# Tree-path attention with a chosen linear layer, four sequences on one core: halves in the first chain, early loads, and denominators summed ahead on VectorE

## The reference, cut to what matters

```python
# 1 conditioned bottleneck, 64 wide, one weight set per sequence
w_down = down_project * (cond @ down_gamma) + cond @ down_beta
h = relu(x @ w_down) @ (up_project * (cond @ up_gamma) + cond @ up_beta) + x
# 2 attention: 8 heads, similarity = shared prefix of 5 soft decisions
paths = sigmoid(h @ Wp + bp)                       # [.., 8 heads, 5]
agree = pq * pk + (1 - pq) * (1 - pk)
sim = cumprod(agree, -1).sum(-1) / 5               # causal mask
x = x + softmax(sim) @ (h @ Wv) @ Wo
# 3 hypernetwork layer, weight of rank 30 per sequence
U = (cond @ W_dec + b_dec).reshape(257, 30)
z = x @ (U @ V)[:-1] + (U @ V)[-1]
# 4 add one of 8 expert products, chosen per token
x = x + z + (z @ expert_w[argmax(z @ gate_w.T)].T)
```

## Time and profile before

| | us |
|---|---|
| median of 3 runs | 155.72 (155.0 to 155.99) |
| the profiled execution | 155.55 |
| its span | 153.4 |
| TensorE busy | 141.2 (92%) |
| VectorE busy | 83.7 (55%) |
| ScalarE busy | 58.8 (38%) |
| GpSimd busy | 31.2 (20%) |

### The profile page before, as it was taken

How to read it: one execution, slowest core, us unless ns; L and a number is a source line. 1 busy time by engine, 2 the same in 40 slices (tenths; PEclk the granted TensorE clock), 3 DMA queues, 4 the chain that set the end, 5 groups by cost and what they waited for, 6 DMA issues and landing times.

```text
span 153.4 us, 5078 instructions
## 1 busy us (share of the span) xinstructions
PE 141.2 (92%) x2296; PEld 89.8 (59%) x2296; DVE 83.7 (55%) x156; ACT 58.8 (38%) x70; POOL 31.2 (20%) x56
## 2 busy tenths in 40 slices
PE   5989678999497999999999999999999999999992
PEld 5746155554274777457656655567558577666650
DVE  0563532619966378296915483558146851985431
ACT  3013156264226342558333451573434447310010
POOL 7200004100405302640022205200222440110000
PEclk9999999999999999999999999999999999999999
DMA  4989999600011200000101000100011010110112
GB/s 121 311 320 433 448 376 353 209 4 0 0 22 17 35 0 4 0 4 0 37 3 38 34 4 0 38 0 4 34 38 38 0 38 0 38 38 34 68 38 71
DMA packets 7381, 12.50 MB, mean 81 GB/s; under 512 B 1552, under 2 KB 5808, under 8 KB 7232
## 3 DMA queue, kind: packets, MB, share of 16 engines
q10 hardware_dynamic: 2496, 7.23, 12.1%
q1 hardware_dynamic: 4768, 4.89, 9.9%
q0 software_dynamic: 96, 0.05, 1.1%
HBM read 9.95 MB, written 2.22 MB: 79 GB/s over the span
## 4 chain that ended last, share of the span: by engine, by line
PE 83%; DVE 11%; ACT 2%; issue 1%; POOL 0%; ACTq 0%; POOLq 0%; DVEq 0%
PE work L561 36%; PE c_ps L561 24%; PE s_ps L561 17%; PE work L738 3%; DVE rden L420 2%; DVE feat L552 2%; PE work L678 2%; DVE tiles L509 1%; ACT prob L365 1%; DVE h_t L455 1%; ACT phi_t L390 1%; DVE u_row L481 1%; PE work L730 1%; DVE x_t L541 1%; DVE logit L464 0%
## 5 line engine op out<-in xcount | busy, mean ns | idle before, releaser
L365 ACT ACTIVATE prob<-s_ps 128x1536 f32<-128x1536 f32 (+1 forms) x24 | 38.2, 1593 | 39.3 <-PE s_ps L561 36.3
L420 DVE RECIPROCAL rden<-c_ps 128x256 f32<-128x256 f32 x16 | 28.1, 1757 | 26.5 <-PE c_ps L561 26.5
L342 POOL TENSOR_SCALAR_AFFINE_SELECT prob<-prob 128x1024 f32<-128x1024 f32 x16 | 20.1, 1257 | 93.1 <-ACT prob L365 93.1
L561 PE MATMUL s_ps<-phi_t 32*128 32x256 f32 (+1 forms) x384 | 24.2, 365 | 1.6 <-ACT phi_t L390 1.0
L561 PE MATMUL c_ps<-prob,v_sb 128*32 128x256 f32 (+1 forms) x384 | 24.9, 346 | 0.0
L561 PEld LDWEIGHTS s_ps<-phi_t 32*128 32x128 f32 x384 | 17.4, 184 | 10.6 <-issue 6.8
L561 PE MATMUL work<-ctx_t,mix_sb 128*32 128x256 f32 x256 | 17.0, 381 | 0.4
L561 PE MATMUL work<-zo_t,gexp 128*32 128x256 f32 x256 | 16.9, 379 | 0.0
L561 PEld LDWEIGHTS c_ps<-prob,v_sb 128*32 128x32 f32 x384 | 11.5, 109 | 9.0 <-issue 2.0
L561 PE MATMUL c_ps<-prob,ones 128*32 128x256 f32 (+1 forms) x256 | 16.3, 326 | 0.0
L561 PE MATMUL work<-w_vl,h_t 128*32 128x296 f32 x208 | 14.8, 416 | 1.1 <-DVE h_t L455 0.6
(11 more groups left out here) (95 smaller groups left out, 133.4 us busy)
## 6 DMA issues: line engine op xcount, KB each, us to landing
wdec<-in_W_dec ACTq DMA_DIRECT2D x1, 3855.0 KB, 15.2
x_t<-in_x_tr SPq DMA_DIRECT2D x4, 512.0 KB, 9.3
ex_t<-in_expert_tr ACTq DMA_DIRECT2D x1, 2048.0 KB, 22.1
out_x<-x_t SPq DMA_DIRECT2D x16, 128.0 KB, 1.7
mix_sb<-in_mix ACTq DMA_DIRECT2D x1, 776.0 KB, 16.8
lift_sb<-in_lift ACTq DMA_DIRECT2D x1, 384.0 KB, 3.7
w_vl<-in_vl SPq DMA_DIRECT2D x1, 296.0 KB, 4.9
first_sb<-in_first SPq DMA_DIRECT2D x1, 144.0 KB, 3.5
```

The source lines that it names most:

```text
L342: nc.gpsimd.affine_select(out=tri, in_=tri, compare_op=ALU.is_ge, fill=0.0, base=0, pattern=[[0, HG], [0, 2], [1, P]], channel_multiplier= ...
L365: nc.scalar.activation(prob[:, p % 2, :, 0:width(p)], s_ps[:, :, 0:width(p)], ACT.Exp).then_inc(exped, 1)
L420: link(nc.vector.reciprocal(rden[:], c_ps[m % 2][:, CW:2 * CW]))
L561: return nc.tensor.matmul(o, w, r, start=start, stop=stop, skip_group_check=True)
```

## The change

The change has four parts. (1) Denominators: in seven of the eight long chunks VectorE now adds all four key tiles into `tiles` (the third whole, of the fourth the half that is not masked), and one block on `tiles`, den(p), makes the whole denominator; it stands one pair later, before the next pair's context, and the normalising follows it. (2) First chain: bias, tanh, feat and phi of sequence 0 run in halves of two token tiles; scores(0) needs only the first; the second half's phi follows scores(1). gdn for sequences 1 to 3 comes before up, gup(1) after it, gup(2) and gup(3) move into the first batch. The phi of head group 1 is now copied by VectorE, for all sequences. (3) Loads: x of sequence 0 is split over both queues, lift_sb comes second on ScalarE's queue, W_dec is split over both and asked for at once. (4) The order list: in sequences 1 to 3 zT, zs and zo come one pair later, zoT and out as well or partly; VL, U and G steps of sequence 0 are dealt out anew. Banks alternate from the other one.

```diff
-WARM = 9
+WARM = 8
-def opening(p):
-    return pair(p)[1][1] == 1 and pair(p)[1][4]
+def adding(p):
+    return pair(p)[1][1] == 1 and p < ALL - 1
 def adds(p):
-    return sum(opening(i) for i in range(p + 1))
+    return sum((1 if pair(i)[1][4] else 2) for i in range(p + 1) if adding(i))
+def closes(p):
+    return pair(p)[1][1] == 1 and pair(p)[1][5] and p < ALL - 1
-PROLOGUE = [("gdn", (0,)), ("gup", 0), ("down", 0), ("gup", 1), ("up", 0, 0), ("up", 0, 1), ("gdn", (1, 2, 3)),
-            ("VL", 0, 0), ("VL", 0, 1), ("VL", 0, 2), ("VL", 0, 3), ("bias", 0), ("tanh", 0), ("feat", 0),
-            ("gup", 2), ("gup", 3), ("phi", 0, 0), ("phi", 0, 1), ("scores", 0), ("down", 1)]
+PROLOGUE = [("gdn", (0,)), ("gup", 0), ("down", 0), ("gdn", (1, 2, 3)), ("up", 0, 0), ("up", 0, 1), ("gup", 1),
+            ("VL", 0, 0), ("VL", 0, 1), *features(0, FIRST), ("VL", 0, 2), ("VL", 0, 3), ("bias", 0, SECOND),
+            ("phi", 0, 0, FIRST), ("phi", 0, 1, FIRST), ("tanh", 0, SECOND), ("scores", 0), ("feat", 0, SECOND),
+            ("down", 1)]
 def after_scores(b):
     if n1 < B:
         gaps[0] += [("up", n1, 0), ("up", n1, 1)]
-        gaps[4] += [("phi", n1, 0), ("phi", n1, 1)]
+        gaps[4] += [("phi", n1, 0, ALL_T), ("phi", n1, 1, ALL_T)]
     if b == 0:
-        gaps[1] += [("VL", n1, 2), ("VL", n1, 3)]
-        gaps[2] += [("U", 1)]
-        gaps[3] += [("U", 3)]
-        gaps[5] += [("G", 1), ("Uadd",)]
+        gaps[0] = [("phi", b, 0, SECOND), ("phi", b, 1, SECOND)] + gaps[0]
+        gaps[1] += [("U", 0)]
+        gaps[2] += [("VL", n1, 2), ("VL", n1, 3)] + features(n1, ALL_T)
+        gaps[3] += [("U", 2)]
+        gaps[5] += [("gup", 3), ("Uadd",)]
     elif n1 < B:
-        gaps[1] += [("zs", prv, ALL_T), ("zo", prv, 0), ("zo", prv, 1), ("VL", n1, 0), ("VL", n1, 1)]
-        gaps[2] += [("VL", n1, 2), ("VL", n1, 3)]
+        gaps[1] += [("VL", n1, 0), ("VL", n1, 1)]
+        gaps[2] += [("zs", prv, ALL_T), ("zo", prv, 0), ("zo", prv, 1), ("VL", n1, 2), ("VL", n1, 3)]
     else:
-        gaps[1] += [("zs", prv, ALL_T), ("zo", prv, 0), ("zo", prv, 1)]
+        gaps[2] += [("zs", prv, ALL_T), ("zo", prv, 0), ("zo", prv, 1)]
         gaps[4] += [("zs", b, FIRST), ("zo", b, 0)]
-    if prv >= 0:
-        gaps[3] += [("zoT", prv, 0), ("zoT", prv, 1)]
+    if prv >= 0 and n1 < B:
+        gaps[5] += [("out", prv, 1)]
 def after_context(b):
     if b == 0:
-        gaps[0] += [("VL", n1, 0), ("VL", n1, 1)]
-        gaps[1] += [("bias", n1), ("tanh", n1), ("U", 0), ("feat", n1)]
-        gaps[2] += [("U", 2)]
-        gaps[3] += [("Q",)]
+        gaps[0] += [("gup", n2)]
+        gaps[1] += [("VL", n1, 0), ("VL", n1, 1)]
+        gaps[2] += [("U", 1)]
+        gaps[3] += [("Q",), ("U", 3)]
         gaps[4] += [("G", 0), ("ubT",)]
-        gaps[5] += [("down", n2), ("WoU",)]
+        gaps[5] += [("G", 1), ("down", n2), ("WoU",)]
     else:
-        gaps[0] += [("zT", prv, ALL_T)]
-        gaps[3] += [("out", prv, 0)]
-        gaps[4] += [("out", prv, 1)]
+        gaps[1] += [("zT", prv, ALL_T)]
+        gaps[3] += [("zoT", prv, 0), ("zoT", prv, 1)]
+        gaps[4] += [("out", prv, 0)]
         gaps[5] += [("out", prv, 2)]
     if prv >= 1:
-        gaps[1] += [("out", prv - 1, 3)]
+        gaps[0] += [("out", prv - 1, 3)]
     if b == B - 1:
         gaps[2] += [("zT", b, FIRST)]
-        gaps[5] = [("zoT", b, 0), ("out", prv, 2), ("out", prv, 3)]
+        gaps[5] = [("out", prv, 1), ("zoT", b, 0), ("out", prv, 2), ("out", prv, 3)]
         if _p + 1 < ALL:
             ORDER += [("scores", _p + 1)]
-        ORDER += _a + [("context", _p)]
+        ORDER += _a
+        if _p and closes(_p - 1):
+            ORDER += [("den", _p - 1)]
+        ORDER += [("context", _p)]
         ORDER += _c
-        if _p + 1 < ALL and opening(_p + 1):
+        if _p + 1 < ALL and adding(_p + 1):
             ORDER += [("add", _p + 1)]
-        _k, _late = _late % 2, _late + 1
+        _k, _late = 1 - _late % 2, _late + 1
 # SyncE
-            sp.dma_start(x_t[:, 0], x_tr[0].rearrange("(c p) t -> p c t", p=P)).then_inc(ld_x[0], 16)
+            sp.dma_start(x_t[:, 0, 0], x_tr[0, 0:P]).then_inc(ld_x[0], 16)
             sp.dma_start(w_vl[:], vl.rearrange("p (c n) -> p c n", c=DC)).then_inc(ld_vl, 16)
-            for b in range(1, B):
-                sp.dma_start(x_t[:, b], x_tr[b].rearrange("(c p) t -> p c t", p=P)).then_inc(ld_x[b], 16)
+            sp.dma_start(wdec[0:P // 2], W_dec[0:P // 2]).then_inc(ld_wdec, 16)
+            sp.dma_start(mix_sb[:], mix).then_inc(ld_mix, 16)
+            sp.dma_start(x_t[:, 2], x_tr[2].rearrange("(c p) t -> p c t", p=P)).then_inc(ld_x[2], 16)
 # ScalarE
+            act.dma_start(x_t[:, 0, 1], x_tr[0, P:2 * P]).then_inc(ld_x[0], 16)
             act.dma_start(lift_sb[:], lift).then_inc(ld_lift, 16)
+            act.dma_start(x_t[:, 1], x_tr[1].rearrange("(c p) t -> p c t", p=P)).then_inc(ld_x[1], 16)
+            act.dma_start(wdec[P // 2:P], W_dec[P // 2:P]).then_inc(ld_wdec, 16)
+            act.dma_start(ex_t[:], expert_tr.rearrange("e (c p) f -> p e c f", p=P)).then_inc(ld_ex, 16)
+            act.dma_start(x_t[:, 3], x_tr[3].rearrange("(c p) t -> p c t", p=P)).then_inc(ld_x[3], 16)
                     if p >= 2:
                         act.wait_ge(summed, p - 1)
-                        if opening(p - 2):
+                        if adding(p - 2):
                             act.wait_ge(added, adds(p - 2))
-                    if s[1] == 0:
-                        act.dma_start(wdec[:], W_dec).then_inc(ld_wdec, 16)
-                        act.dma_start(mix_sb[:], mix).then_inc(ld_mix, 16)
-                        act.dma_start(ex_t[:], expert_tr.rearrange("e (c p) f -> p e c f", p=P)).then_inc(ld_ex, 16)
 # VectorE: gdn in one multiply and one add for all its sequences
+                elif kind == "phi" and s[2] == 1:
+                    nc.vector.tensor_scalar(phi_t[:, b % 2, g, tok], bank(s)[:, tok], rootc[:], None, op0=ALU.mult
+                                            ).then_inc(empty(s), 1)
-                    if pair(p)[1][5]:
+                    if pair(p)[1][5] and not closes(p):
                         dve.wait_ge(summed, p + 1)
                         normalise(chunk(p))
+                elif kind == "den":
+                    dve.wait_ge(closed, closings(s[1]))
+                    normalise(chunk(s[1]))
                 elif kind == "add":
-                    nc.vector.tensor_tensor(tiles[:, chunk(p) % 2], both[:, :, 0, :], both[:, :, 1, :], ALU.add
-                                            ).then_inc(added, 1)
+                    if pair(p)[1][4]:
+                        dve.wait_ge(exped, p + 1)
+                        nc.vector.tensor_tensor(acc, both[:, :, 0, :], both[:, :, 1, :], ALU.add).then_inc(added, 1)
+                    else:
+                        dve.wait_ge(masked, masks(p))
+                        dve.wait_ge(added, adds(p) - 2)
+                        nc.vector.tensor_tensor(acc, acc, both[:, :, 0, :], ALU.add).then_inc(added, 1)
+                        dve.wait_ge(added, adds(p) - 1)
+                        nc.vector.tensor_tensor(acc[:, :, P:CW], acc[:, :, P:CW], both[:, :, 1, 0:P], ALU.add
+                                                ).then_inc(added, 1)
 # TensorE
+            def denominators(p):
+                m = chunk(p)
+                pe.wait_ge(added, adds(p))
+                for h in range(HG):
+                    ins = mm(c_ps[m % 2][DH * h:DH * (h + 1), CW:2 * CW], ones[:], tiles[:, m % 2, h, :],
+                             start=False, stop=(p < ALL - 1))
+                return ins
-                if half and last:
-                    pe.wait_ge(added, adds(p))
-                    for h in range(HG):
-                        mm(c_ps[m % 2][DH * h:DH * (h + 1), CW:2 * CW], ones[:], tiles[:, m % 2, h, :],
-                           start=False, stop=False)
+                if p == ALL - 1:
+                    denominators(p)
-                    if half and first:
+                    if half and p < ALL - 1:
                         continue
```

More of the change, by code:

```diff
@@ L147 @@
           ("out", B - 1, 1), ("zoT", B - 1, 1), ("out", B - 1, 2), ("out", B - 1, 3)]
-NO_BANK = ("scores", "context", "add", "bias", "tanh", "feat", "Uadd", "zo")
+NO_BANK = ("scores", "context", "den", "add", "bias", "tanh", "feat", "Uadd", "zo")
 EARLY = 6
@@ L260, in build @@
         added = sem("added")
+        closed = sem("closed")
         ctx_ready = sem("ctx_ready")
@@ L578, in scores @@
                 if p % BP < NG:
-                    done(pe, ("phi", b, g))
+                    done(pe, ("phi", b, g, ALL_T if b else FIRST))
+                elif b == 0 and first:
+                    done(pe, ("phi", b, g, SECOND))
                 for i, (kt, q0, n) in enumerate(units):
@@ L629, in _ @@
                     context(s[1])
+                    continue
+                if kind == "den":
```

(7 more changed lines are left out.)

84 lines of the change are left out of this document (48 added, 36 removed).

## The result

The changed kernel takes 190.18 us (median of 4 runs, 189.20 to 192.08) beside 155.53 for the kernel before (four runs, one more than in the table above): a ratio of 1.221, 95% interval 1.214 to 1.228. I had forecast 155.7, with a range of 153.0 to 158.0. The profiled execution has a span of 187.8 us and a device time of 189.94, 34.4 us above its counterpart of before.

What follows compares the result with a forecast made beforehand. It took TensorE's attention work, the start of the first scores and VectorE's in-order delivery as the bound. Terms -2.1 + 0.4 + 0.4 + 1.5 = +0.2 us on 155.55 gave 155.7 us, range 153.0 to 158.0.

Steps and rivals of the forecast that it cites:

- The other moves cost and give nothing: Remaining moves, among them W_dec asked for 6 us earlier but wanted only 20 us later: no cost, no gain.
- The early loads hurt: Rival: lift_sb or bp_b lands late, first chain gains 1 us less or more; 156.7 to 157.6 us, chance 0.06.
- Part 1: Denominators: TensorE loses 4.5 us of work, VectorE gets 13.3 us of adds, some 100 us in all, mostly hidden.
- Part 2: First chain: first VL at 11.1, S(0) at 17.2 instead of 21.31, but up(1,0) only 1.95 us earlier.
- Part 3: Rest of the first batch: moved gups +1.7, closings -1.3, waits -0.6; -2.1 us up to S(7), earlier start included.
- Part 4: Choice path one pair later: longer waits on VectorE; +0.4 us each in batches 1 and 2, +1.5 in batch 3.
- wait for pick: Batches 1 and 2: TensorE waits 1.4 to 1.9 us before the fourth VL, whose bank pick releases.
- Batch 3: Last batch: waits at zoT and before out(2,2), sum +1.2, or +2.3 if zo lets add(21) pass; taken +1.5 us.
- The cut stays: Rival: the choice path's waits don't grow, so TensorE's saving remains; 150.2 to 154.1 us, chance 0.29.
- GpSimd and VectorE hold each other: Rival: added adds collide with masks and zo, +1.0 us in each of two to four stages; 157.7 to 159.7, chance 0.21.
- its sign of 1.8 us: Sign of the contention rival: several VectorE adds lasting 1.8 us or more.

Runs made afterwards that it cites:

- e1: The changed kernel with the loads as in the kernel before, so only the changed order of work: 162.22 us, 160.00 at full clock.
- e8: e1 with three order moves: VL(b+1,2) ahead of zs in batches 1 and 2, out(1,3) ahead of zoT(2), out(2,1) ahead of context 23: 156.87 us.
- e9: e8 with U(2) right behind U(1) and batch 0's second-half phi copies on VectorE instead of ScalarE: 154.61 us.
- e13: e9, but the chunk that pair 21 closes keeps the old denominators, so six chunks have the second adds: 152.32 us.
- e3: The changed kernel with batch 3's token load issued last on SyncE instead of sixth on ScalarE: 167.23 us.
- e11: e9 with the denominators of the kernel before (no second adds, no later closing): 157.89 us over 13 runs, 155.45 to 155.78 at full clock.
- e12: e9 with the changed early loads, but W_dec in one piece and the experts last: 155.73 us.
- e7: e1 with the denominators of the kernel before (no second adds, no den step): 162.80 us, 159.42 at full clock.
- e10: The changed kernel with ScalarE's last two loads swapped, batch 3's tokens fifth and the experts last: 166.57 us, one run.
- e4: e3 with W_dec as one load over all 128 partitions on ScalarE's queue instead of two halves: 162.79 us.

## Why the prediction was wrong, point by point

The profiled executions at full clock, by the start of scores: S(p) and the end of the span, in us.

| | S(0) | S(7) | S(13) | S(19) | end |
|---|---|---|---|---|---|
| before | 21.31 | 55.18 | 84.74 | 115.03 | 153.4 |
| e1, the order alone | 18.09 | 54.00 | 84.17 | 115.74 | 157.9 |
| e8 | 16.79 | 52.86 | 81.91 | 112.36 | 152.9 |
| e9 | 18.02 | 52.43 | 81.49 | 111.94 | 152.5 |
| e13 | 17.37 | 51.70 | 80.75 | 111.20 | 150.2 |

**The step that failed** is the one under "The other moves cost and give nothing": "W_dec, asked for 6 us earlier, is wanted by the first U only 20 us later". I asked when the data would be there, and not what the *issues* do to the engine that makes them. Five loads were put ahead of ScalarE's first Relu, and I costed none of them. At 0.5 us each they would indeed have been free. One took 29.49 us, and with it went 27 of the 34 us: S(0) stands at 45.48 in the changed kernel and at 18.09 in e1. The rival "The early loads hurt" had the right part of the change and the wrong mechanism: late data, priced at 1 us, chance 0.06. The late data exist as well, by the cut of W_dec, but in e3 they cost 4.4 us (167.23 against 162.79), and in the changed kernel they hide behind the longer wait. No row of before showed a long issue. Still, a bound from rows was to be had: W_dec's own load took 15 us, and an issue that waits for it costs as much.

**Part 1.** VectorE's load is as computed, 100.6 us in e1 against "some 100", and the added adds take 1.22 and 0.69 us each, as taken from the earlier trace rows. TensorE's busy time fell less than its 4.5 us: to 138.3 in e1, at full clock, from 141.2. Of the other 1.6 us, 0.9 is the first gup, 1.91 us long instead of the 1.05 of the earlier trace rows; in e8, where it took 1.02, TensorE is busy 137.4, 3.8 less than before. The rest I didn't follow. In time part 1 as a whole is worth 1.4 us (e11).

**Part 2.** The mechanism is right and the start a little off: S(0) at 18.09 instead of 17.2, because the first VL came at 11.93 instead of 11.1, which the long first gup accounts for; in e8 both came earlier than forecast (10.65 and 16.79). `up(1,0)` waits for ScalarE's phi copy, as I wrote, 1.35 us against 1.5. In e12 and in the changed kernel lift_sb landed after 4.7 to 4.9 us against 3.7, a wait of 0.3 to 0.4, as put in "5.3 to 6.2".

**Part 3.** From S(0) to S(7) I had 35.9 us, e1 took 35.91. U(3) came at 41.73 behind a wait of 1.45 (forecast 41.3 and 1.7). The 0.9 us missing up to S(7) (-1.2 instead of -2.1) are the later start. That the stretch agrees to 0.1 us is partly luck, since two terms were off and cancel: gup(2) and gup(3) cost 1.05 each and not 0.86, 0.4 more, and den(5), 0.43 us, stands behind S(7) in the new order while before it stood ahead, which I hadn't counted.

**Part 4.** The wait for pick came where and as forecast: 1.7 us each, 1.45 more than the 0.24 of the earlier trace rows, against 1.4 "extra wait". Batch 1 cost +0.6 (forecast +0.4), batch 2 +1.3. e8 removes both waits, and from S(0) on it is 3.7 us shorter, so the argument by VectorE's order holds. Of the 0.7 by which batch 2 is worse than batch 1, half is a wait of 0.34 us that only batch 2 has, of a VL for VectorE's add to x_t at 92.31; for the other half I have no row. Batch 3 is the mis-sized term: +3.8 against +1.5. Of the 3.8, 0.4 is moved work: den(17) now stands behind S(19). I had left open whether zo would let add(21) pass, had priced that at 1.1 us and taken 0.3 of it. It does wait, and for three adds where I had counted one: the four zo take 4.67 instead of 2.34, with waits of 1.8 and 1.5 at zoT where I had 0.4 and 0.7. The wait before out(2,2) is 0.63 against 0.75. In e7, e11 and e13, which have no add(21), the four zo take 2.33 or 2.34 again, which shows these adds to be the cause.

**The rivals.** "The cut stays" doesn't hold in this order: its condition, that the waits of part 4 don't grow, was not met (3.4 us for pick, 3.3 for zo). e8 meets it for pick and still waits 2.0 us for zo; at 155.0 us it lies above that rival's 154.1. e13 waits for neither and lands at 152.3, inside its range. "GpSimd and VectorE hold each other" was right in its mechanism and named zo as a place, but not in where and how much: it had 1.0 us in each of two to four stages, and e1 shows one stage with some 2.3 us. The masks, its other place, last 1.15 us on the mean in e1 and lasted 1.26 before, so they are not held more than they were, and no VectorE add in e1 reaches its sign of 1.8 us (the longest is 1.57). That the order alone, 160.0 at full clock, comes near its 157.7 to 159.7 is luck to that extent. I gave it 0.21 and should have given it more: the sum itself left a price of 1.1 us open at one of its places.

## What to carry to other kernels

An issue of a DMA is an instruction of the engine that makes it: before loads are put ahead of an engine's first work, ask what each waits for, put the load with the most rows last, and have no other behind it on the same queue. Don't cut a load by partitions over two queues to make it faster; here it made it slower. And when work is moved to VectorE, look which GpSimd instruction with two SBUF inputs runs at that moment and whether TensorE waits for it; leave the adds out there, and keep them elsewhere.

## What the runs showed of the hardware

- An issue on ScalarE's queue lasted 29.49, 28.75, 21.64 and 18.93 us where it stood behind the experts' load (2048 rows of 1 KB, 1024 in the third) with W_dec ahead of that; with the experts last, in e10 and e12, no issue took more than 0.82 us. In e3 SyncE issued seven loads, none of them the experts', in under 0.6 us each.
- The same loads moved at 172 to 248 GB/s in e3, with W_dec cut into 64 and 64 partitions on two queues, and at 331 to 475 in e4, uncut on one.
- Four zo of 128x256 on GpSimd take 2.34 us undisturbed and 4.67 in e1 beside three VectorE adds with two SBUF inputs. Of these the first, of 128x1024, keeps its 1.22 us, the 128x512 takes 0.99 instead of 0.69 and the last, of 128x1024, 1.57 instead of 1.22. In e9 each zo that meets an add ends 0.47 or 0.48 us after that add.
- The granted clock falls to half (1.2 GHz) for some microseconds after TensorE has stood still, in some executions of a kernel and not in others. The five executions of e11 at full clock lie within 155.45 to 155.78 us, the eight others at 157.82 to 158.69. In its profiled execution TensorE had stood 3.01 us before a matmul group that then ran 1.94 us instead of 1.08, at a granted clock of 0.50 from 54.6 to 57.4 us. In e1, e7 and e8 too the executions at a lower clock took 2 to 4 us longer. e13, whose longest wait after the start is 0.8 us, kept 0.999 or more in five runs. A long wait doesn't always cost the clock: the kernel before, with one of 2.2 us, was at 0.989 in 4 of the 57 executions measured along with the experiments, and those 4 took 156.19 to 156.32 us, while the others took 154.97 to 156.44.
